# Last expert layer with inner units on partitions and tokens along the free side, token weights repeated by DMA, and weights split expert by expert

## What is computed

```python
logits = xt @ Wr.T + bias                    # xt: 1024 tokens x 256, E = 16
probs = softmax(logits)
topk_val, topk_idx = top_k(probs, 2)
w = topk_val / (sum(topk_val) + EPS)
g = einsum('th,ehi->tei', xt, Wg)            # i = 128
u = einsum('th,ehi->tei', xt, Wu)
y = einsum('tei,eih->teh', silu(g) * u, Wd)
routed = einsum('tke,tk,teh->th', one_hot(topk_idx), w, y)
shared = silu(xt @ sWg) * (xt @ sWu) @ sWd
x = x + routed + shared                      # xt is the layer norm of x
```

## Time and profile before

| | us |
|---|---|
| median of the runs shown | 2011.44 (2011.28 to 2013.61, 3 runs) |
| the profiled execution | 2012.85 |
| its span, first to last instruction | 2011.0 |
| TensorE matmuls busy | 1543.9 (77%) |
| VectorE busy | 1142.4 (57%) |
| ScalarE busy | 564.2 (28%) |
| GpSimd busy | 336.9 (17%) |
| mean granted TensorE clock, share of 2.4 GHz | 0.889 |

### The profile page before, as it was taken

One profiled execution on the slowest core, in us unless ns is written; L12 is line 12 of the kernel. 1 busy time (PEld: TensorE's weight loads), 2 busy tenths in 40 slices (PEclk: granted clock), 3 DMA queues, 4 the chain that ended last, 5 costly groups with the idle time before them and its releaser, 6 DMA issues. The chain is left out here.

```text
span 2011.0 us, 22678 instructions
## 1 busy us (share of the span) xinstructions
PE 1543.9 (77%) x8004; PEld 1097.0 (55%) x8004; DVE 1142.4 (57%) x2040; ACT 564.2 (28%) x1083; POOL 336.9 (17%) x183
## 2 busy tenths in 40 slices
PE   6899999992999632865892756656767899937998
PEld 3467667681999512554772212222455455527998
DVE  4566666408333667343334799799545677664343
ACT  0033333203222221201221233333133355532222
POOL 0000000005000000102004346356273000040000
PEclk9999999995999866977996879989988899976999
DMA  1200002202000200022442012112000233000000
GB/s 55 66 11 16 16 10 88 59 0 68 0 0 0 84 0 0 0 86 100 162 141 84 22 42 73 52 52 73 21 14 1 59 97 89 18 0 1 0 0 21
DMA packets 72686, 84.76 MB, mean 42 GB/s; under 512 B 7576, under 2 KB 61463, under 8 KB 72496
## 3 DMA queue, kind: packets, MB, share of 16 engines
q1 hardware_dynamic: 71088, 79.93, 12.8%
q0 software_dynamic: 1536, 4.00, 0.6%
HBM read 70.41 MB, written 7.41 MB: 39 GB/s over the span
## 5 line engine op out<-in xcount | busy, mean ns | idle before, releaser
L818 POOL TENSOR_TENSOR rstd<-var_eps,half_neg 128x8 f32<-128x8 f32 x11 | 18.1, 1646 | 1107.6 <-DVE var_eps L1816 1101.1
L1987 DVE SCALAR_TENSOR_TENSOR f_h<-f_silu,f_weight,psum 128x128 f32<-128x128 f32 (+1 forms) x232 | 75.5, 365 | 204.4 <-ACT f_silu L1612 204.4
L1334 PE MATMUL psum<-m_state_c,ident 128*128 128x512 f32 x256 | 131.4, 637 | 69.4 <-POOL m_state_c L880 69.4
L880 POOL TENSOR_TENSOR m_state_c<-m_state,m_c 128x1024 f32<-128x1024 f32 x64 | 150.6, 2353 | 154.3 <-DVE m_state L2263 154.3
L2263 DVE TENSOR_TENSOR_SCAN m_state<-m_decay,psum 128x512 f32<-128x512 f32 x128 | 149.2, 1208 | 4.8
L1123 PE MATMUL psum<-f_gate_up_high,f_x_high 128*128 (+2 forms) x464 | 141.6, 305 | 0.0
L1123 PE MATMUL psum<-f_gate_up_low,f_x_high 128*128 (+2 forms) x464 | 140.6, 303 | 0.0
L1123 PE MATMUL psum<-f_gate_up_high,f_x_low 128*128 (+2 forms) x464 | 140.5, 303 | 0.0
L2360 DVE TENSOR_REDUCE a_max_pieces<-psum 128x4 f32<-128x512 f32 (+2 forms) x176 | 108.2, 639 | 50.9 <-PE psum L1446 31.3
L1750 ACT ACTIVATE a_probT<-psum 128x512 f32<-128x512 f32 (+1 forms) x176 | 97.3, 558 | 88.9 <-PE psum L1473 85.3
L1334 PEld LDWEIGHTS psum<-m_state_c,ident 128*128 128x128 f32 x256 | 45.5, 197 | 134.8 <-POOL m_state_c L880 101.5
(11 more groups left out here) (378 smaller groups left out, 3510.1 us busy)
## 6 DMA issues: line engine op xcount, KB each, us to landing
f_fc<-in_L_ffn_fc_w_dram SPq DMA_DIRECT2D x16, 1024.0 KB, 7.7
m_c<-m_c_rows SPq DMA_DIRECT2D x32, 512.0 KB, 3.6
f_gate_up<-in_L_ffn_w_up_gate_dram SPq DMA_DIRECT2D x2, 1408.0 KB, 8.6
wq<-in_L_attn_Wq_dram SPq DMA_DIRECT2D x16, 128.0 KB, 2.2
wkv<-in_L_attn_Wk_dram SPq DMA_DIRECT2D x16, 128.0 KB, 2.2
wkv<-in_L_attn_Wv_dram SPq DMA_DIRECT2D x16, 128.0 KB, 2.2
wo<-in_L_attn_Wo_dram SPq DMA_DIRECT2D x1, 2048.0 KB, 8.7
f_slot_rows<-f_taken SPq DMA_DIRECT2D x1, 2048.0 KB, 8.7
```

What stands on the lines that cost most here:

```text
L880: pool.tensor_tensor(hc2[c][:], h2[c][:], c_wide[v][:].rearrange("p (b s) -> p b s", b=BATCH), ALU.mult).then_inc(s_hc, 1)
L1334: mm = pe.matmul(bank[2 * c + b], ident[:], hc2[c][:, b, :], start=False, stop=True, skip_group_check=True)
L1987: ins = dve.scalar_tensor_tensor(g.h[j % 2][:, e * g.hidden:(e + 1) * g.hidden], g.silu[j % 2][:, e, :], g.weight[:, half * ST + j, bass.d ...
```

## The change

Only the last gated layer changes; `ffn0` keeps the old form.

- **Layout.** For one expert and one batch (a step; 17 x 2 = 34 steps, the shared expert first for both batches, then batch 0's and batch 1's sixteen) the weights are stationary and 512 tokens move: 12 fp32r matmuls of 512 columns give gate and up with the inner units on partitions. silu and product give h already in the form that the down product needs as stationary operand. No transposes.
- **Down** is 4 plain fp32 matmuls of 256 columns for each step, in PSUM banks 0 to 3, with h and the raw down weights unsplit.
- **Shares.** A token's weight now lies along the free side, so it has to be repeated on all partitions. TensorE turns the shares into `shareT` (16 x 1024), SP stores it to DRAM and loads one row of 512 for each step, spread over 128 partitions, into one of three buffers. VectorE multiplies h by it in a second operation. The two shared steps have none.
- **Split.** ScalarE rounds and VectorE subtracts the weights of one expert at a time, two steps ahead (`wide_high`, `wide_low`); ScalarE's `high_parts` and GpSimd's `low_parts` for this layer are gone.
- **Router.** 4 fp32 matmuls of 512 columns with the router stationary, bias added by ScalarE, and 8 small transposes back. The choice of experts is made between the first steps.
- **Start and end.** x's parts are made batch by batch and feature tile by feature tile, from PSUM where possible. x is added in four pieces and stored by four DMAs.

The diff, with declarations cut:

```diff
@@ sync
-            sp.wait_ge(ffn3.s_res, 8)
-            sp.dma_start(out.rearrange("b (j p) d -> p (b j) d", p=P), x[:]).then_inc(s_out, 16)
-            sp.wait_ge(s_out, 16)
+            sp.wait_ge(s_cols, 3 + BATCH)
+            sp.dma_start(share_rows, shareT[:]).then_inc(s_cleared, 16)
+            sp.wait_ge(s_cleared, 48)
+            g = ffn3
+            for s, (e, b, m) in enumerate(g.steps):
+                if m is not None:
+                    if m >= WB:
+                        sp.wait_ge(s_wh_mul, g.step0 + s - WB + 1)
+                    sp.dma_start(g.share[m % WB][:], share_rows[e:e + 1, b * SEQ:(b + 1) * SEQ].broadcast_to([P, SEQ])
+                                 ).then_inc(s_wb[m % WB], 16)
+            for c in range(4):
+                sp.wait_ge(s_res, ADDED["f3"] - 3 + c)
+                sp.dma_start(out.rearrange("b (j p) d -> p (b j) d", p=P)[:, 2 * c:2 * c + 2], x[:, 2 * c:2 * c + 2]).then_inc(s_out, 16)
+            sp.wait_ge(s_out, 64)
@@ gpsimd
-                if n == 10:
-                    low_parts(ffn3)
@@ tensor
+            def wide_up(g, s):
+                e, b, _ = g.steps[s]
+                pe.wait_ge(s_wl, g.high0 + s + 1)
+                if s >= 2:
+                    pe.wait_ge(s_wh_mul, g.step0 + s - 1)
+                for c in range(2):
+                    for n, (k, w_, x_) in enumerate(TERMS_W):
+                        mm = pe.matmul(bank[4 + 2 * (s % 2) + c], g.w[w_][s % 2][:, k, c * P:(c + 1) * P],
+                                       g.x[x_][:, k, b * SEQ:(b + 1) * SEQ], start=(n == 0), stop=(n == len(TERMS_W) - 1))
+                mm.then_inc(s_wgu, 1)
+            def wide_down(g, s):
+                e, b, _ = g.steps[s]
+                pe.wait_ge(s_wh_mul, g.step0 + s + 1)
+                for j in range(ST):
+                    mm = pe.matmul(bank[2 * b + j // 2][:, (j % 2) * DM:(j % 2 + 1) * DM], g.h[s % 2][:, j * P:(j + 1) * P],
+                                   g.dn[:, e // 2, e % 2, :], start=False, stop=True, skip_group_check=True)
+                mm.then_inc(s_wdown, 1)
@@ tensor, experts3
-                route(g, 5, bias_row)
-                pe.wait_ge(g.s_w, 16 * (12 + 15))
-                gated_layer(g)
+                pe.wait_ge(s_xT0, 12)
+                pe.wait_ge(s_xT1, 12)
+                pe.wait_ge(g.s_router, 16 * g.turn)
+                for b in range(BATCH):
+                    for k in range(KT):
+                        mm = pe.matmul(bank[6 + b][0:EXPERTS3], g.router[:, k, :], xnT[:, k, b * SEQ:(b + 1) * SEQ],
+                                       start=(k == 0), stop=(k == KT - 1))
+                mm.then_inc(g.s_logits, 1)
+                pe.wait_ge(s_xhi, 9)
+                pe.wait_ge(s_xlo, 9)
+                wide_up(g, 0)
+                pe.wait_ge(s_cols, 2 + BATCH)
+                for j in range(TT):
+                    mm = pe.transpose(bank[3][:, j * EXPERTS3:(j + 1) * EXPERTS3], logitsT[:, j * P:(j + 1) * P],
+                                      ident[0:EXPERTS3, 0:EXPERTS3])
+                mm.then_inc(g.s_count, 1)
+                wide_up(g, 1)
+                for c in range(2):
+                    open_sums(c)
+                wide_down(g, 0)
+                wide_up(g, 2)
+                pe.wait_ge(g.s_weight, g.turn)
+                for j in range(TT):
+                    mm = pe.transpose(bank[2 + j // ST][0:EXPERTS3, (j % ST) * P:(j % ST + 1) * P], g.tmp[2][:, j, :], ident[:])
+                mm.then_inc(s_cols_mm, 1)
+                pe.wait_ge(s_cols, 3 + BATCH)
+                for c in range(2, 4):
+                    open_sums(c)
+                wide_down(g, 1)
+                for s in range(3, len(g.steps)):
+                    wide_up(g, s)
+                    wide_down(g, s - 1)
+                wide_down(g, len(g.steps) - 1)
@@ scalar
-            high_parts(ffn3, 8)
-            act.wait_ge(ffn3.s_diff, ffn3.turn)
-            act.activation(ffn3.small[1][:], ffn3.small[0][:], ACT.Exp).then_inc(ffn3.s_exp, 1)
-            gated_layer(ffn3)
+            def experts3():
+                g = ffn3
+                act.wait_ge(s_res, ADDED["a3"])
+                act.wait_ge(g.s_w, 16 * g.loads)
+                wide_high(g, 0)
+                for b in range(BATCH):
+                    o = slice(b * SEQ, (b + 1) * SEQ)
+                    act.wait_ge(s_turn, KT * BATCH * 8 + KT * b + 1)
+                    act.copy(xnT[:, 0, o], bank[2 * b]).then_inc(s_xT0, 1)
+                    act.copy(g.x[0][:, 0, o], bank[2 * b]).then_inc(s_xhi, 1)
+                    act.wait_ge(s_xT1, 10 + b + 1)
+                    act.copy(g.x[0][:, 1, o], xnT[:, 1, o]).then_inc(s_xhi, 1)
+                wide_high(g, 1)
+                act.wait_ge(s_w1, LOADED["f3_router"])
+                act.wait_ge(g.s_logits, g.turn)
+                for b in range(BATCH):
+                    act.activation(logitsT[:, b * SEQ:(b + 1) * SEQ], bank[6 + b][0:EXPERTS3], ACT.Identity, bias=bias_col[:]).then_inc(s_cols, 1)
+                for s in range(len(g.steps)):
+                    wide_silu(g, s)
+                    if s + 2 < len(g.steps):
+                        wide_high(g, s + 2)
+                    if s == 0:
+                        act.wait_ge(g.s_diff, g.turn)
+                        act.activation(g.small[1][:], g.small[0][:], ACT.Exp).then_inc(g.s_exp, 1)
@@ vector
+            def wide_mul(g, s):
+                e, b, m = g.steps[s]
+                dve.wait_ge(s_wsilu, g.step0 + s + 1)
+                if s >= 2:
+                    dve.wait_ge(s_wdown, g.step0 + s - 1)
+                ins = dve.tensor_tensor(g.h[s % 2][:], g.silu[s % 2][:], bank[5 + 2 * (s % 2)], ALU.mult)
+                if m is not None:
+                    ch.step(ins)
+                    ch.sync()
+                    dve.wait_ge(s_wb[m % WB], g.share0[m % WB] + 16 * (m // WB) + 16)
+                    ins = dve.tensor_tensor(g.h[s % 2][:], g.h[s % 2][:], g.share[m % WB][:], ALU.mult)
+                ins.then_inc(s_wh_mul, 1)
@@ vector, experts3
-                ln_copy(8)
-                low_x(g)
-                choose(g, positions=False)
-                clear(g)
-                dve.tensor_copy(g.weight[:, :, 0:g.routed], g.tmp[2][:]).then_inc(g.s_weight, 1)
-                dve.wait_ge(g.s_weight, g.turn)
-                gated_layer(g)
+                wide_low(g, 0)
+                for b in range(BATCH):
+                    o = slice(b * SEQ, (b + 1) * SEQ)
+                    dve.wait_ge(s_turn, KT * BATCH * 8 + KT * b + 2)
+                    dve.tensor_copy(xnT[:, 1, o], bank[2 * b + 1]).then_inc(s_xT1, 1)
+                    dve.wait_ge(s_xT0, 10 + b + 1)
+                    dve.wait_ge(s_xT1, 10 + b + 1)
+                    for k in range(KT):
+                        dve.wait_ge(s_xhi, 4 + KT * b + k + 2)
+                        dve.tensor_tensor(g.x[1][:, k, o], xnT[:, k, o], g.x[0][:, k, o].bitcast(F32), ALU.subtract).then_inc(s_xlo, 1)
+                wide_low(g, 1)
+                dve.wait_ge(g.s_count, g.turn)
+                ch.step(dve.tensor_copy(g.logits[:], bank[3][:, 0:TT * g.routed].rearrange("p (j e) -> p j e", j=TT)))
+                ch.sync()
+                pick_two(g)
+                dve.tensor_tensor(g.small[0][:], g.top[:, :, 1], g.top[:, :, 0], ALU.subtract).then_inc(g.s_diff, 1)
+                wide_mul(g, 0)
+                wide_low(g, 2)
+                shares(g)
+                dve.wait_ge(s_cols_mm, 5)
+                dve.tensor_copy(shareT[:].rearrange("p (b s) -> p b s", b=BATCH), psum[0:EXPERTS3, 2:4, :]).then_inc(s_cols, 1)
+                for s in range(1, len(g.steps)):
+                    wide_mul(g, s)
+                    if s + 2 < len(g.steps):
+                        wide_low(g, s + 2)
+                for c in range(4):
+                    dve.wait_ge(s_wdown, g.step0 + len(g.steps) - (1 if c < 2 else 0))
+                    o = x[:, 2 * c:2 * c + 2, :]
+                    dve.tensor_tensor(o, o, bank[c].rearrange("p (j d) -> p j d", j=2), ALU.add).then_inc(s_res, 1)
```

More of the change, by code:

```diff
@@ L573, in build @@
         s_wo3_mm = sem("a3_out_product")
-        ffn3 = gated("f3", 16, 1, 128, w_odd.fresh(), ffn0)
+        class Wide:
+            pass
+        TERMS_W = [(k, *parts) for k in range(KT) for parts in ((0, 0), (0, 1), (1, 0))]
+        s_wh, s_wl, s_wgu, s_wsilu, s_wh_mul, s_wdown = s_g_high, s_g_low, gated_sems[1], gated_sems[2], gated_sems[3], gated_sems[4]
+        WB = 3
+        s_wb = [gated_sems[5], gated_sems[6], s_hT_low]
+        ffn3 = Wide()
+        EXPERTS3, HID3 = 16, 128
+        w, wo_ = work.fresh(), w_odd.fresh()
+        ffn3.gu = wo_.take("f3_gate_up", [P, KT, EXPERTS3 + 1, 2 * HID3])
+        ffn3.dn = wo_.take("f3_down", [P, EXPERTS3 // 2 + 1, 2, DM])
+        ffn3.s_w, ffn3.loads = gated_sems[0], 12 + 15
+        ffn3.x = [w.take(f"f3_x_{c}", [P, KT, TOK], F32R) for c in ("high", "low")]
```

(58 more changed lines are left out.)

6 lines of the change are left out of this document (4 added, 2 removed).

## The result

The changed kernel takes 1961.83 us (median of 4, 1961.23 to 1963.32) against 2011.74 for the kernel before, a ratio of 0.975 with a 95% interval of 0.973 to 0.977. It is 50 us faster, not 73: the time lies above the predicted range (1929 to 1953). The profiled span is 1960.2 us; 1937.8 was predicted for it.

What follows compares the result with a forecast made beforehand. TensorE was taken to bound the expert part, after a start held up by GpSimd beside VectorE. Start -41.5, expert part -30.7 and end -1 gave -73.2 us, so 1938 us from 2011.44; range 1929 to 1953.

Steps and rivals of the forecast that it cites:

- from there to the end of down(2): First steps, from the first gate-and-up's end to the third down product's end, choice of experts between: 17.9 us forecast.
- the price of a down call: Down product of each step: 4 plain fp32 matmuls of 256 columns at 0.219 us each, 0.88 us a step.
- second rival: Down product: plain fp32 matmuls cost double, 136 x 0.219 = +30 us, 1968 us; chance 2%.
- four in 3.75: Router: profile row read as four fp32 matmuls of 512 columns in 3.75 us, 0.85 each at 1.2 GHz.
- four ups and three downs: First steps: gate-and-up and down products reckoned at 13.7 us, leaving 4.2 us over the plain steps for choosing experts.
- the clock loss: Pauses of TensorE at the start lower its clock: two taken at 1.7 us, 3.4 us lost; bounds 0 and 7.
- the last wait: End of the expert part: the last down product waits 1.5 us for its chain of 2.4 us.
- The hole at the start: Layer start: xn held beside GpSimd's low parts loses 27 us; without them it falls from 29.6 to 2.67 us.
- rival 3: Layer start doesn't shrink, because xn is slow for another reason than GpSimd: +27 us, 1965 us; chance 3%.
- The chain beside the step: ScalarE and VectorE work behind each gate-and-up: 2.4 us, hidden under TensorE's 3.64 us with 1.2 us of slack.
- rival 1: Expert steps: VectorE's chain becomes the bound; at 4.1 us a step, +15 us, 1954 us; chance 8%.
- rival 4: Expert part: TensorE's clock stays at 1.2 GHz through pauses in each step; 6.9 us a step, +111, 2049 us; chance 2%.

## Why the prediction was wrong, point by point

The predicted and the profiled span, 22.4 us apart, by the prediction's own steps:

| step | predicted | measured | difference |
|---|---|---|---|
| xn starts at | 1786.5 | 1785.1 | -1.4 |
| xn to the end of up(0) | 13.0 | 14.5 | +1.5 |
| from there to the end of down(2) | 17.9 | 20.3 | +2.4 |
| 30 ups, 31 downs, last wait, clock | 114.9 | 136.2 | +21.3 |
| the end | 5.5 | 4.1 | -1.4 |

**The step that failed is the price of a down call**, "fp32 on both sides: 32 in 7.17 us ... 0.219 us each". The row is right, and 0.219 us is the distance between its records. But its loop makes 8 tiles x 2 = 16 calls. The 32 records were taken for 32 calls, and the price per record was multiplied by the number of calls. Down costs 1.73 us a step and not 0.88; 34 x 0.85 = 29 us. The prediction's second rival had this mechanism and the sum 1968, and was given 2 in 100, on the strength of "32 rows of just this shape". By the rule of the Trainium skill cited in the prediction (FP8 and Floating Point Precision, TensorE Precision Notes) a plain fp32 call takes four passes. The trace does agree: 0.43 us for 256 columns at 2.4 GHz is four column times, in two records of two, and an fp32r call with 0.12 us is about one.

The same mistake stands a second time in the router: "four in 3.75" are records too, so four calls took 5.66 us where 3.4 were reckoned, five of the distances 0.85 us at 1.2 GHz. And a third time in the "48 small ones" that they replace: 8 tiles with three matmuls each are 24 calls, and 48 records.

A slip beside it left the sum as it was: up to down(2) the first steps hold three ups and three downs, 10.9 us at the predicted prices, and not "four ups and three downs", 13.7. So 7.0 us over the plain steps were forecast there, not 4.2, and 6.9 were measured (20.3 - 3 x 4.46).

With both put right the sum would have been 1937.8 + 28.9 + 2.3 = 1969. It is 1960.2 because smaller terms were too large: the clock loss (3.4 us on top; a mean clock of 0.93 in the 25.4 us behind up(0) is some 1.8 us, and it lies inside the 20.3 us), the last wait (1.5; measured 0.4, which hangs on the price too, since with half of the calls it is 1.27), gate and up (0.227 a call and not 0.230, 1 us in sum), the end (1.4), and the earlier start (1.4).

**What was right.** The hole at the start went as forecast: xn fell to 2.67 us, with GpSimd's work as its cause (rival 3 is out: dose and effect in three kernels). The first expert product came ahead of the choice of experts, and gate and up cost what was forecast. The chain beside the step stayed hidden: idle time of TensorE is zero even at 3.22 us a step, with the chain that was reckoned at 2.4, so rival 1 is out with more room than was claimed. The loads of the shares were hidden but for VectorE's wait before step 2, which cost TensorE nothing. The clock was at 1.00 in the steady part, so rival 4 is out; its trigger, a pause in each step, never came.

**Where the 50 us are.** Start: from rstd to the first expert product 51.3 to 11.6, -39.8. The kernel without the low parts splits it: 27.0 of them are GpSimd's (24.4 are left there), of the other 12.8, 7.0 are the choice of experts (from the logits on VectorE, 1801.16, to 1808.15), which up(0) no longer waits for, and 6.4 are the router, 5.6 us in four wide calls where 24 small ones took 12.0; it starts 0.6 us later. That gain of the wide router was not forecast as a term of its own. Part of it is the clock: 0.50 through all of the 12.0 us, but 0.82 in the last 2.2 of the 5.6. Expert part: from there to the last additions 167.0 (1837.82 to 2004.85) to 159.5 (1796.68 to 1956.16), -7.5. End: 6.2 to 4.0, -2.1. The layer starts 1.4 earlier. In sum 50.8, as the spans. The step itself went from 4.92 us (83.8 + 83.5, by 34) to 4.46, -0.46 x 34 = -16; half of that goes on the choice of experts, which now lies inside the part (159.5 - 34 x 4.46 = 7.9). Of the 31 us forecast for the expert part the larger share was lost to the plain product: at 3.64 us a step it would have been 28 more.

## What to carry to other kernels

Before a row's time is divided, count the calls that the loop in the code makes, and check that count against the row's; where a rule and a row differ by a factor of two, the count is the suspect. Three fp32r products of split operands cost TensorE less than one plain fp32 product of the same shape (0.36 against 0.43 us). Each place where the splitting stands in a chain gives part of that back, here about 1 us in the last step. A long GpSimd operation can hold what VectorE needs next between SBUF tiles: moved behind one victim, it found the next. What kept its speed beside it here were copies out of PSUM, MAX8 and the index searches.

## What was not expected of the hardware

A plain fp32 matmul leaves two records, each two column times apart (0.216 us for 256 columns at 2.4 GHz). VectorE's MAX8 and its copies out of PSUM aren't held by GpSimd (0.71 us for eight and 0.69 each), while a cast of 16 columns was, for 3.79 us. TensorE's waits of 0.5 and 1.3 us in the 29 us behind the router stood with a mean clock of 0.94 there, in the changed kernel and in the one with the first two steps plain; where one wait of 1.2 us was left, the clock stayed at 1.00. But it stayed at 1.00 too in the kernel with half of the down calls, with waits of 0.4, 1.3 and 1.6 us in its 29 us:

```profile
1797.40:1826.40 29.00, 25.62 (x118) 19.42 (x118) 14.71 (x51) 11.93 (x18) 0.00 (x0) 1.00 0.20 57
```

So the waits alone don't tell whether the clock falls; what does stays open.
